# ScalarE's half of the adjacency loads issued by GpSimd from the third unit on, in a graph attention layer

## The reference

```python
def _L0_gnn_ref(h, adj, W, a):
    Wh = h @ W
    s1 = Wh @ a[:OUT_F, 0]
    s2 = Wh @ a[OUT_F:, 0]
    e = jax.nn.leaky_relu(s1[:, None] + s2[None, :], negative_slope=0.2)
    attention = jax.nn.softmax(jnp.where(adj > 0, e, -9e15), axis=1)
    return jax.nn.elu(attention @ Wh)

h = jnp.maximum(_layernorm(x, axis=-1), 0.0)
return x + _L0_gnn_ref(h, adj, L0_gnn_W, L0_gnn_a)
```

## Time and profile before

| | |
|---|---|
| time, median of 3 runs (lowest, highest) | 1016.66 us (1013.93, 1019.99) |
| the profiled execution's own time | 1015.67 us |
| its span, first to last instruction | 1014.0 us |
| mean granted clock of PE | 0.984 |
| busy: PE, DVE, ACT, POOL | 956.4, 842.2, 529.2, 52.4 us |
| bytes moved | 280.73 MB, mean 277 GB/s |

### The profile page before, as it was taken

How to read it: one execution, slowest core, us unless ns; L and a number is a source line. 1 busy time by engine, 2 the same in 40 slices (tenths; PEclk the granted TensorE clock), 3 DMA queues, 4 the chain that set the end, 5 groups by cost and what they waited for, 6 DMA issues and landing times.

```text
span 1014.0 us, 21306 instructions
## 1 busy us (share of the span) xinstructions
PE 956.4 (94%) x8432; PEld 952.1 (94%) x8432; DVE 842.2 (83%) x833; ACT 529.2 (52%) x363; POOL 52.4 (5%) x138
## 2 busy tenths in 40 slices
PE   4649879999999999999999999999999999999996
PEld 4649879999999999999999999999999999999996
DVE  5737767989888998889888998889888898889885
ACT  4546655465445645455545654556455654546420
POOL 3613220000000000000000000000000000000000
PEclk9869999999999999999999999999999999999998
DMA  9999999999999999999999999999999999999800
GB/s 264 290 286 270 213 212 253 264 309 295 353 283 293 269 318 331 297 291 272 354 299 290 268 322 327 294 295 265 352 298 302 259 324 329 294 294 276 246 0 24
DMA packets 276946, 280.73 MB, mean 277 GB/s; under 512 B 9697, under 2 KB 272033, under 8 KB 276897
## 3 DMA queue, kind: packets, MB, share of 16 engines
q1 hardware_dynamic: 140816, 144.53, 53.8%
q10 hardware_dynamic: 136080, 135.58, 49.9%
HBM read 275.84 MB, written 4.23 MB: 276 GB/s over the span
## 4 chain that ended last, share of the span: by engine, by line
PE 90%; SPq 4%; DMA 3%; issue 2%; DVE 1%; ACT 0%; ACTq 0%
PE ps L1003 88%; DMA raw<-in_adj 3%; SPq L184 2%; SPq L193 1%; PE ps L975 1%; PE ps L965 0%; PE ps L1012 0%; DVE big L826 0%; DVE big L837 0%; DVE obuf L840 0%; ACT gate L444 0%; SPq L214 0%; DVE big L834 0%; SPq L204 0%; ACT big L409 0%
## 5 line engine op out<-in xcount | busy, mean ns | idle before, releaser
L1003 PE MATMUL ps<-wh,weights 128*128 (+1 forms) x8192 | 923.4, 276 | 8.0 <-DVE weights L724 8.0
L1003 PEld LDWEIGHTS ps<-wh,weights 128*128 128x128 f32 x8192 | 921.3, 193 | 9.0 <-issue 6.8
L724 DVE SCALAR_TENSOR_TENSOR weights<-big,beta 128x1024 f32<-128x1024 f32 x512 | 646.4, 1275 | 128.8 <-PE ps L1003 126.9
L444 ACT ACTIVATE gate<-raw 128x4096 uint8<-128x4096 int32 x126 | 456.5, 3623 | 405.9 <-DVE big L708 386.4
L708 DVE STREAM_TRANSPOSE big<-gate 128x1024 int32<-128x1024 int32 x127 | 157.1, 1237 | 4.1 <-ACT gate L444 3.9
L975 PE MATMUL ps<-wext,big 128*128 128x130 f32 x128 | 19.7, 308 | 12.3 <-issue 11.6
L975 PEld LDWEIGHTS ps<-wext,big 128*128 128x128 f32 x128 | 17.8, 217 | 13.7 <-issue 13.7
L471 ACT ACTIVATE big<-ps,rden 128x128 f32<-128x128 f32 x56 | 23.1, 412 | 12.2 <-issue 12.2
L671 DVE TENSOR_TENSOR wh<-ps,wh 128x512 f32<-128x512 f32 x16 | 10.8, 674 | 15.3 <-ACT beta L421 15.3
L472 ACT ACTIVATE big<-ps,rden 128x128 f32<-128x128 f32 x56 | 23.4, 418 | 0.0
L965 PE MATMUL ps<-identf,obuf 128*128 128x128 f32 x32 | 6.5, 349 | 16.1 <-ACT obuf L401 15.7
(11 more groups left out here) (92 smaller groups left out, 113.7 us busy)
## 6 DMA issues: line engine op xcount, KB each, us to landing
raw<-in_adj ACTq DMA_DIRECT2D x256, 512.0 KB, 10.8
raw<-in_adj SPq DMA_DIRECT2D x256, 512.0 KB, 10.8
out_x<-obuf SPq DMA_DIRECT2D x28, 128.0 KB, 10.7
xs<-in_x SPq DMA_DIRECT2D x24, 128.0 KB, 11.5
big<-r_rows SPq DMA_DIRECT2D x6, 512.0 KB, 14.0
xs<-in_x ACTq DMA_DIRECT2D x8, 128.0 KB, 4.6
out_x<-obuf SPq DMA_DIRECT2D x4, 64.0 KB, 1.7
out_x<-obuf ACTq DMA_DIRECT2D x4, 64.0 KB, 2.0
```

Of the source, the lines that this page charges most:

```text
L444: nc.scalar.activation(gate[:, u % GATE_SLOTS, :, :], raw[:, u % RAW_SLOTS, :, :], ACT.Sign)\
L724: nc.vector.scalar_tensor_tensor(weights[:, v % WT_SLOTS, :], rbc[:, half, :], beta[:, bass.ds(jt, 1)], turned_bytes[:, chunk, v // QUAD, ...
L1003: ins = nc.tensor.matmul(acc[half][:, t // BANK_TILES, t % BANK_TILES, 0:FD], weights[:, u % WT_SLOTS, t * P:(t + 1) * P], moving, start=s ...
```

## The change

Units 0 and 1 are loaded as before. From unit 2 on POOL issues groups 2 and 3, and they count on semaphores of their own, `pool_in`, one for each slot; `raw_in` then gets 32 for a unit and not 64. ACT loses `load_next` and `load_ahead`, and its pass waits for both semaphores. POOL issues units 2 and 3 right after its normalisations of chunk 2; then, in the safe path, `load_next` waits for the pass of unit u - 4 and issues unit u, for all u of the first band, with `late_variances` of chunks 3 to 7 put in after units 5, 7, 9, 11 and 13. The later bands are a loop of 16 such loads. SP's part is unchanged in the safe path.

```diff
         raw_in = [sem(f"raw_in{k}") for k in range(RAW_SLOTS)]
+        pool_in = [sem(f"pool_in{k}") for k in range(RAW_SLOTS)]
         r_stored, r_in = sem("r_stored"), sem("r_in")
...
 
-        def load_unit(eng, band, unit, groups):
+        def load_unit(eng, band, unit, groups, landed=raw_in):
             chunk, half = unit // 2, unit % 2
...
                 eng.dma_start(raw[group * SQ:(group + 1) * SQ, slot, :, :].rearrange("p (b q) j -> p b q j", q=4),
-                              rows.rearrange("x b k q j -> x b (k q) j")).then_inc(raw_in[slot], 16)
+                              rows.rearrange("x b k q j -> x b (k q) j")).then_inc(landed[slot], 16)
 
...
             normalise(EARLY, 1)
-            for n in range(EARLY + 1, CHUNKS):
-                late_variances(n)
-            base = links[0]
+            for u in range(2, RAW_SLOTS):
+                load_unit(pool, 0, u, (2, 3), pool_in)
+            common = links[0]
+
+            def safe_path():
+                def load_next(band, u):
+                    pool.wait_ge(gate_ready, band * UNITS + (u - RAW_SLOTS + 1))
+                    load_unit(pool, band, u, (2, 3), pool_in)
+
+                for u in range(RAW_SLOTS, UNITS):
+                    load_next(0, u)
+                    if u % 2 == 1 and EARLY + u // 2 - 1 < CHUNKS:
+                        late_variances(EARLY + u // 2 - 1)
+                with pool.Fori(1, BANDS) as band:
+                    for u in range(UNITS):
+                        load_next(band, u)
+
 
...
                 LINKS = 3
+                links[0] = common
+                for n in range(EARLY + 1, CHUNKS):
+                    late_variances(n)
+                base = links[0]
                 pool.sem_inc(g_hacc_free, 2)
...
             with pool.If(safe(pool)):
+                safe_path()
                 pool.nop()
...
                     turn = u // RAW_SLOTS + 1
-                    act.wait_ge(raw_in[u % RAW_SLOTS], band * (UNITS // RAW_SLOTS * 64) + turn * 64)
+
+                    slot = u % RAW_SLOTS
+                    first = 32 if slot < 2 else 0
+                    act.wait_ge(raw_in[slot], band * (UNITS // RAW_SLOTS * 32) + (turn * 32 + first))
+                    act.wait_ge(pool_in[slot], band * (UNITS // RAW_SLOTS * 32) + (turn * 32 - first))
                     if not isinstance(band, int) or band * UNITS + u >= GATE_SLOTS:
...
                         .then_inc(gate_ready, 1)
-
-                def load_next(band, u):
-
-                    act.wait_ge(gate_ready, band * UNITS + (u + 1))
-                    ahead = u + RAW_SLOTS
-                    load_unit(act, band + ahead // UNITS, ahead % UNITS, (2, 3))
 
...
 
-                def load_ahead(u):
-
-                    ahead = u + AHEAD
-                    if ahead >= RAW_SLOTS:
-                        act.wait_ge(gate_ready, ahead - RAW_SLOTS + 1)
-                    load_unit(act, ahead // UNITS, ahead % UNITS, (2, 3))
-
                 def first_band():
...
                     first_words(0, 0, first_gates)
-                    load_ahead(0)
                     relu(2)
...
                     first_words(1, 1, gate_ready)
-                    load_ahead(1)
                     source_factors(2)
...
                         form_gates(0, u)
-                        if u < UNITS - 1:
-                            load_ahead(u)
                         n = u // 2
...
                             normalise(n + 1, 1)
-                        if u == UNITS - 2:
-                            load_ahead(u + 1)
-                        if u == UNITS - 1:
-                            load_ahead(u + 1)
-                            load_ahead(u + 2)
 
...
                                 store_rows()
-                        if u + RAW_SLOTS < UNITS or not last:
-                            load_next(band, u)
                         if u == 6:
```

More of the change, by code:

```diff
@@ L259, in general_path @@
             def general_path():
-                for k in range(RAW_SLOTS):
+                for k in range(2):
                     sp.wait_ge(raw_in[k], 64)
@@ L562, in general_path @@
             def general_path():
-                for u in range(2, RAW_SLOTS):
-                    load_unit(act, 0, u, (2, 3))
                 for n in range(1, CHUNKS):
@@ L881, in general_path @@
                 for k in range(2, RAW_SLOTS):
-                    dve.wait_ge(raw_in[k], 64)
+                    dve.wait_ge(raw_in[k], 32)
+                    dve.wait_ge(pool_in[k], 32)
                 here = links[0]
```

## The result

The changed kernel takes 1228.72 us (median of 4 runs, 1224.76 to 1271.56), the kernel before 1015.29 us beside it (4 runs, 1013.48 to 1019.99). The ratio is 1.2072, with a 95% interval of 1.2039 to 1.2104: slower by a fifth, far above the range of the prediction. One run of the four, 1271.56, is from a disturbed execution: it counts in the median, but not in the ratio. The profiled execution took 1224.76 us, its span is 1223.1 us.

What follows compares the result with a forecast made beforehand. PE was taken to bound the seven later bands, leaving only the start to gain. Terms -2.6 + 0 + 0 + 0 = -2.6 us gave 1014 us (from the median 1016.66), range 1009 to 1045.

Steps and rivals of the forecast that it cites:

- Edit 6: Later bands: a unit takes 7.16 us and needs two POOL issues, so issues up to 3.58 us keep pace; worth 0.
- X: Time of one POOL load issue, in no earlier trace; taken as 1.6 us, bounded by 0.586 and 4.982 us.
- Rival (e): POOL's issues hold up DVE (1165 us) or the DMA engines, with a margin of an eighth; chance 0.08.
- Edit 5: Price of one POOL issue: ACT's median 0.64 us plus 0.99 for one collision with DVE, 1.6 us.
- Edit 4: First band: eight POOL issues ahead of chunk 3's variances cost 0 if each takes below 2.4 us.
- (c): POOL late for the variances, with issues of 3.0 to 3.58 us: 1019 to 1026 us; chance 0.10.
- (d): POOL becomes the bound from issues of 3.58 us on: 1041 to 1328 us; chance 0.12.
- Edit 1: ACT no longer issues 252 of its 256 loads, 162 us of sequencer time; in the later bands worth 0.
- Edit 2: Start: POOL issues units 6 and 7, free of ACT's waits; unit 6's pass starts at 72.2, not 74.75: -2.6 us.
- Edit 3: Start: POOL issues units 2 and 3 later; unit 2's pass 3.6 us late, hidden in stalls: 0, within 1.5 us.
- (b): The whole start moves, unit 4 also landing some 3 us earlier: -5.6 us, 1011 us; chance 0.15.
- (a): Start: SP's half of unit 6 was last anyway and lands no earlier: 1015 to 1018 us; chance 0.17.

## Why the prediction was wrong

**Edit 6, "X up to 3.58 us keeps pace", is the step that failed.** It costed the issue, and took 10.8 us for the landing from ACT's row, as if a load issued in time landed in time. X was 0.774 us, far inside its limit, and the bands still got longer by 27.5 us each (192.7 / 7). What was late was not POOL's half but SP's, whose row I read as unchanged because the change doesn't touch it. While POOL's half came in, SP's queue moved 60 GB/s, a unit took 8.7 us in place of 7.16, and SP's loads landed after 22.1 us in the median. The two experiments that undo one condition each, 4 KB rows on SP (1028.13) and all partitions (1014.05), and the one that makes the loss without GpSimd (1210.83), carry this.

**Rival (e)** named the place in its last sentence, "packets of the new queue are slower", and then gave the margin of an eighth and no time; it had 0.08 together with the stall of DVE. That margin was all that stood between the forecast and a loss: 303 needed and 347 possible with even shares, but 235 moved. The rate of one queue alone, 201 GB/s, stood in the rows too, and I read it as the rate of one *queue*. It is the rate of one half of the partitions: one queue over all of them moved 300. With that reading, a unit in which SP's queue gets a fifth could have been priced from the rows of before, had the packet size of the new queue been known. No row of before shows it.

**Edit 5** (X = 1.6 us) was twice what was measured, 0.774 in the median. The collision with DVE hardly came; the longest issue is 1.30, and a weighing of DVE took 1271 ns in the mean (1273 before), so the first part of rival (e) fell. The Trainium skill (SBUF — State Buffer, Who interferes with whom) infers that an operation of DVE with two inputs does not keep GpSimd from writing descriptors; the trace agrees, with no issue above 1.30 us. **Edit 4** held as a price: eight issues took 6.01 us, POOL's variances of chunk 3 were done at 40.1 us, and X was below 2.4. But it counted POOL alone. The seeds reached POOL at 54.29 us, and not by about 50, because DVE stood for unit 2's pass. Rivals **(c)** and **(d)** hung on X alone and fell with it.

**Edit 1** held: ACT lost its issues and waited for other things. **Edit 2** was right in its mechanism and wrong in its worth. By itself it moves unit 6 by 3.9 us, not 2.6, and the end by nothing; "PE gets it all" failed against POOL's wait and the clock. In the change it did not even come to bear: POOL issued unit 6 at 61.81 us and not at about 57, later than ACT's 59.04, and 57 to 66 us had 237 GB/s in place of over 300.

**Edit 3** (0, within 1.5 us) failed. It put unit 2's landing at 32.1 + X + 6 = 40 us, and the first packet came after 39 us, 6.3 us behind the issue; unit 2's pass began 11.5 us late and not 3.6; and it gave SP's queue about half of the rate once both are filled. Its reason that SP's queue sets unit 4's landing was right, as the run with x later shows, and for that very reason the small share moved unit 4 by 14.4 us. **Rival (b)** took the same place for a gain and fell; with SP's queue truly relieved it is real, and worth 5.2 us.

Rival **(a)**, that SP's half would come last anyway, was the nearest in kind. It was priced for one unit at the start and with half of 347 GB/s; it was true of every unit.

## What to carry to other kernels

When a load moves to another issuer, price what it does to the loads that stay: look at the packet size of each queue (bytes by packets in the queue table) and at the partitions that each stream fills. Streams that must land together should have packets of one size, or each fill all 128 partitions; a margin in GB/s holds only for the shares under which it was measured. And when a load is late, look first at what stands ahead of it on its own queue.

## What the runs showed of the hardware

- Queues take turns by the packet: 116 to 115 packets with 4 KB against 1 KB, 88 to 86 with 4 KB each, 110 to 106 with 4 KB against 2 KB, 131 to 130 between two hardware queues, 69 to 69 with loads over all partitions.
- GpSimd's queue joined four rows of 1 KB into a packet of 4096 bytes; the rows did not have to lie together in the partition.
- Loads that fill partitions 0 to 63 alone came in at 207 GB/s; the same queue with loads over all 128 partitions at 300, and 350 in the start. The Trainium skill (DMA: Bandwidth & Descriptors, Rules for kernel authors) advises against two transfers to disjoint halves because they serialize. Here two such streams moved 347 GB/s together and one 201, so they did not.
- From GpSimd's issue to the first packet of its queue over 6 us passed at the start: issue at 32.66, no packet until 39 us. In a later band the issue of 408.10 us has its first packets after 413 us; there it is hidden, as POOL issues four units ahead.
- A GpSimd issue of 512 KB took 0.774 us in the median beside a busy DVE.
